# DLRM tower on one Trainium2 core: fifteen tables looked up by one-hot matmul instead of five, and pair products kept in four chunks instead of seven

## The chip, the cores and the metric

One core of one Trainium2 chip runs the kernel, compiled as one program. The metric is the device time of one execution in microseconds (us): the median over runs. The kernel before takes 226.08 us (three runs, 224.97 to 227.42).

## The reference

```python
# ids: (512, 26) int32; 26 tables of 1000, 1250, 12500 or 125000 rows x 128; dense: (512, 128)
e = stack([tbl_n[ids[:, n]] for n in range(26)], axis=1)           # (512, 26, 128)
combined = concatenate([dense[:, None, :], e], axis=1)               # 27 features per sample
interactions = einsum('bfd,bgd->bfg', combined, combined)            # 27 x 27 products per sample
z = concatenate([dense, interactions[:, iu, ju]], axis=1)            # the 351 pairs f < g
h = concatenate([z, dense], axis=1)                                  # 607 columns
h = maximum(h @ W_top1 + b_top1, 0); h = maximum(h @ W_top2 + b_top2, 0)   # 607x512, 512x256
y = h @ W_top3                                                       # (512, 1)
```

All of it is fp32.

## The kernel before

The batch of 512 is four tiles of 128 samples. Everything ends in `featT` (128 dims on the partitions, sample, feature), from which the products of one sample are one small matmul.

There are two ways into `featT`. **Gathered tables** (21 of 26): GpSimd issues one indirect DMA per tile and table (84 in all, L289), which fetches 128 rows to `gathered`; TensorE transposes them in groups of up to four tables (`fill`, L485), and ScalarE or VectorE copies the group to `featT` (L307, L385). **One-hot tables** (5, of 1000 rows): the table lies in SBUF as 125 partitions with 8 rows each; for each of the 8 chunks a one-hot matrix (row number equals id) is made, and table chunk times one-hot, accumulated in PSUM over the chunks, is the looked-up embedding, already transposed, for all 512 samples. To be exact, the table is split in a high part (ScalarE, L333) and a low part (VectorE, L424), so each chunk is two matmuls (L462, L464). The ids are spread over the partitions: by a small matmul (L475) for VectorE, which compares three chunks in an instruction (L418, six chunks of eight), and by DMA for ScalarE, which does the other two with an Abs (L347) and a Relu (L352). ScalarE then copies the result to `featT` (L301).

SP issues the loads in its program's order (`load_table`, L253, waits for a free one of three buffers); GpSimd issues the gathers without waiting for anything but the ids.

Then come five stages: tiles 0 to 2, and tile 3 in two (columns cut at chunk 5). In a stage, TensorE computes the 128 products of a tile (L511, four quadrants of the array), VectorE and ScalarE copy them from PSUM to `zT` (L391, L314), in seven chunks of at most 122 rows, and layer 1 multiplies `zT` by `w_inter` (L539) and adds the dense part (L534, which reads `featT` at feature 0). Layers 2 and 3 (L563, L573) follow a tile later. Each fp32 matmul shows as two instructions in the profile, so 128 products are 256. The order of TensorE's work is written out at the end of its program, with `BESIDE` blocks of layer 1 of the stage before placed between quarters of the products. Engines meet only in semaphores.

## Time and profile before

| | us |
|---|---|
| time, median of 3 runs | 226.08 (224.97 to 227.42) |
| profiled execution, span from first to last instruction | 152.9 |
| profiled execution, its own time | only its span is shown |
| TensorE matmuls busy | 115.3 (75%) |
| weight loads busy | 95.1 (62%) |
| VectorE busy | 51.1 (33%) |
| ScalarE busy | 49.8 (33%) |
| GpSimd busy | 83.9 (55%) |
| bytes moved by DMA | 12.82 MB, mean 84 GB/s |

A busy time is the sum of an engine's instructions; what the busy share hides is that the span has two parts with different limits, which the views by stretch and the chain of waits tell apart. In a row of instructions, `out<-in` names the tiles, `x40` the count; behind the bar stand busy us, mean ns of one, and the idle time of the engine before them with what ended it.

### The profile page before, as it was taken

To read this page: it belongs to the slowest core of one execution; us is meant where nothing else is said; L and a number is where in the kernel's file an instruction comes from. 1 tells how busy PE (TensorE), PEld (TensorE's weight loads), DVE (VectorE), ACT (ScalarE), POOL (GpSimd) and SP (SyncE) were. 2 spreads that over 40 slices of the span, in tenths; PEclk is the share of its full clock that TensorE was granted. 3 is DMA by queue.
4 is the path that set the end of the run, shared out by engine and by line. 5 is a ranking of instruction groups with operands and counts; after the bars stand their busy time and mean duration, and the time that the engine had idled before them with its cause. 6 is when DMAs were issued, how large, how long until landed. Compare 5 with 4: busy or idle time off the path is not lost.

```text
span 152.9 us, 3980 instructions
## 1 busy us (share of the span) xinstructions
PE 115.3 (75%) x1789; PEld 95.1 (62%) x1789; DVE 51.1 (33%) x88; ACT 49.8 (33%) x98; POOL 83.9 (55%) x91
## 2 busy tenths in 40 slices
PE   0339401999379965599899899958999949995993
PEld 0127201677157654486788788647989739994691
DVE  6665600076457810712103800234500405104100
ACT  5045203368499840703000800204500106104011
POOL 4777777777787877777777777777710000000000
PEclk9999955569978999557999999997799996999659
DMA  1684447999644322221222221122210000000000
GB/s 43 151 192 164 166 164 227 270 248 238 172 166 167 119 53 57 50 57 51 55 53 56 58 51 51 51 56 56 60 30 0 0 9 0 4 4 0 4 0 1
DMA packets 5547, 12.82 MB, mean 84 GB/s; under 512 B 2025, under 2 KB 3049, under 8 KB 5277
## 3 DMA queue, kind: packets, MB, share of 16 engines
q0 software_dynamic: 2688, 5.51, 15.2%
q1 hardware_dynamic: 2832, 7.05, 15.0%
q8 instruction: 14, 0.23, 0.7%
q14 instruction: 3, 0.02, 0.0%
q10 hardware_dynamic: 10, 0.01, 0.0%
HBM read 12.56 MB, written 0.00 MB: 82 GB/s over the span
## 4 chain that ended last, share of the span: by engine, by line
PE 57%; DMA 25%; DVE 7%; issue 7%; ACT 2%; SPq 1%; ACTq 0%
DMA table_sb<-tbl 25%; PE h_ps L539 17%; PE gram_ps L511 9%; PE h_ps L563 7%; PE h_ps L534 6%; PE fill_ps L485 5%; DVE zT L391 5%; PE gram_ps L462 3%; PE gram_ps L539 3%; PE gram_ps L464 3%; DVE featT L385 2%; ACT featT L301 1%; PE gram_ps L534 1%; PE h_ps L573 1%; DVE h L396 1%
## 5 line engine op out<-in xcount | busy, mean ns | idle before, releaser
L289 POOL DMA_INDIRECT gathered<-tbl,ids_sb x84 | 83.1, 989 | 26.9 <-issue 25.3
L539 PE MATMUL h_ps<-zT,w_inter_sb 122*128 122x128 f32 (+1 forms) x196 | 29.2, 295 | 1.6 <-DVE zT L391 1.6
L539 PEld LDWEIGHTS h_ps<-zT,w_inter_sb 122*128 122x128 f32 (+1 forms) x196 | 27.3, 203 | 4.7 <-DVE zT L391 1.9
L462 PE MATMUL gram_ps<-onehot,table_hi 125*128 125x512 f32 x40 | 20.8, 519 | 4.8 <-DVE table_lo L424 4.7
L314 ACT ACTIVATE zT<-gram_ps 26x224 f32<-26x224 f32 (+4 forms) x40 | 12.1, 302 | 37.7 <-PE gram_ps L511 36.9
L418 DVE TENSOR_TENSOR onehot<-h_ps,rowno 125x1536 fp32r<-125x1536 f32 x10 | 17.5, 1755 | 17.8 <-PE gram_ps L464 16.9
L511 PE MATMUL gram_ps<-featT 128*26 128x26 f32 (+2 forms) x1280 | 15.5, 188 | 9.0 <-issue 5.8
L391 DVE COPY zT<-gram_ps 26x224 f32<-26x224 f32 (+4 forms) x40 | 12.9, 323 | 24.6 <-PE gram_ps L511 23.5
L511 PEld LDWEIGHTS gram_ps<-featT 128*26 128x26 f32 (+1 forms) x1280 | 13.2, 102 | 11.9 <-issue 7.5
L464 PE MATMUL gram_ps<-onehot,table_lo 125*128 125x512 f32 x40 | 19.6, 490 | 0.0
L307 ACT ACTIVATE featT<-fill_ps 128x512 f32<-128x512 f32 (+1 forms) x14 | 9.1, 656 | 26.4 <-PE fill_ps L485 26.4
L385 DVE COPY featT<-fill_ps 128x512 f32<-128x512 f32 (+1 forms) x10 | 6.0, 605 | 31.4 <-PE fill_ps L485 31.4
L485 PE MATMUL fill_ps<-ident,gathered 128*128 128x128 f32 x84 | 13.4, 302 | 3.7 <-ACT featT L307 3.4
L462 PEld LDWEIGHTS gram_ps<-onehot,table_hi 125*128 125x128 f32 x40 | 10.2, 254 | 9.6 <-DVE table_lo L424 5.4
L485 PEld LDWEIGHTS fill_ps<-ident,gathered 128*128 128x128 f32 x84 | 10.8, 157 | 5.7 <-issue 5.1
L563 PE MATMUL h_ps<-h,w_sb 128*128 128x128 f32 x64 | 13.2, 390 | 0.1
L563 PEld LDWEIGHTS h_ps<-h,w_sb 128*128 128x128 f32 x64 | 12.3, 295 | 0.4 <-issue 0.2
L534 PE MATMUL h_ps<-featT,w_dsum 128*128 128x128 f32 x28 | 10.4, 463 | 2.5 <-DVE zT L391 2.5
L464 PEld LDWEIGHTS gram_ps<-onehot,table_lo 125*128 125x128 f32 x40 | 10.1, 253 | 2.3
L347 ACT ACTIVATE id_off<-oh_ids_sb,minus_rowno 125x512 f32<-125x512 int32 x10 | 7.2, 717 | 10.8 <-DMA oh_ids_sb<-oh_ids 10.6
L333 ACT ACTIVATE table_hi<-table_sb 125x1024 fp32r<-125x1024 f32 x5 | 5.3, 1053 | 12.6 <-DMA table_sb<-tbl 12.6
L424 DVE TENSOR_TENSOR table_lo<-table_sb,table_hi 125x1024 fp32r<-125x1024 f32 x5 | 6.1, 1223 | 6.2 <-ACT table_hi L333 6.2
(33 smaller groups left out, 55.5 us busy)
## 6 DMA issues: line engine op xcount, KB each, us to landing
table_sb<-tbl SPq DMA_DIRECT2D x5, 500.0 KB
w_inter_sb<-w_inter SPq DMA_DIRECT2D x1, 1792.0 KB, 29.9
gathered<-tbl,ids_sb POOLq DMA_INDIRECT x84, 3.8
oh_ids_sb<-oh_ids SPq DMA_DIRECT2D x1, 1000.0 KB
w_dense_sb<-w_dense SPq DMA_DIRECT2D x1, 512.0 KB, 25.0
w_sb<-w SPq DMA_DIRECT2D x1, 512.0 KB, 26.8
dense_sb<-dense SPq DMA_DIRECT2D x1, 256.0 KB, 23.2
oh_ids_sb<-oh_ids SPq DMA_DIRECT2D x1, 250.0 KB
```

The costliest lines, as they stand in the source:

```text
L289: pool.indirect_dma_start(out=gathered[:, t, pos - GATHERED[0], :], out_offset=None, in_=tables[table], in_offset=bass.IndirectOffsetOnAxi ...
L307: nc.scalar.activation(group_target(t, g), group_source(n % 2, g), ACT.Copy) \
L314: nc.scalar.activation(z_target(stage, j, q), z_source(stage, j, q), ACT.Copy) \
L391: nc.vector.tensor_copy(z_target(stage, j, q), z_source(stage, j, q)).then_inc(z_dve, 1)
L418: nc.vector.tensor_tensor(onehot[:, c:c + DVE_STEP, :], oh_ids_ps(k).unsqueeze(1).to_broadcast(of_step), rowno[:, c:c + DVE_STEP].unsqueez ...
L462: nc.tensor.matmul(lookup_ps(k), table_hi[:, k % 2, rows], onehot[:, c, :], start=(c == 0), stop=False)
L464: last = nc.tensor.matmul(lookup_ps(k), table_lo[:, k % 2, rows], onehot[:, c, :], start=False, stop=(c == RCHUNKS - 1))
L485: last = nc.tensor.transpose(fill_ps[n % 2][:, i * P:(i + 1) * P], gathered[:, t, pos - GATHERED[0], :], ident[:, :])
L511: last = nc.tensor.matmul(gram_ps[stage % 2][QUAD * j:QUAD * j + rows, col + first:col + rows], featT[:, b, 0:rows], featT[:, b, 1 + first ...
L534: nc.tensor.matmul(layer1_ps(t, n), w_dsum[:, units], featT[:, tile, 0], start=(n == 0 or (t == LAST and n == N1 // 2)), stop=False, skip_ ...
L539: last = nc.tensor.matmul(layer1_ps(t, n), w_inter_sb[0:k, c, units], zT[0:k, c, tile], start=False, stop=(c == CHUNKS - 1), skip_group_ch ...
L563: last = nc.tensor.matmul(h2_ps[:, n * P:(n + 1) * P], w2_sb[:, k, n * P:(n + 1) * P], h1[:, k, :], start=(n == 0 and k == 0), stop=(k == ...
```

## The change

Fifteen tables instead of five are looked up by one-hot matmul: the twelve of 1000 rows (8 chunks) and three of 1250 rows (10 chunks), all padded with zeros by the host to 128 partitions. The remaining eleven are gathered, 44 gathers instead of 84, and a gather is held back until a count of looked-up chunks is reached (`chunks_ahead`). The ids are spread by DMA for each table ahead of its rows; ScalarE makes a second copy with one added, and VectorE compares two chunks in one instruction on SBUF operands alone (`compare_two`). Lookups are written to PSUM in pairs of banks and copied to `featT` in pairs of features (`pair_to_featT`); `featT` has 32 slots, five of them second copies of features (`COPIED`). The products of a sample are 32 rows by 27 columns, and because some rows are there twice, the 351 pairs are picked with two copies per quadrant (`BELOW`, then `ABOVE` over its first `CUT` rows) into four full chunks of `zT` instead of seven; `w_inter` is laid out to match. The dense input has its own `denseT`. Tile 3 is no longer cut in two stages; TensorE's order behind the lookups is a written list; layer 3 runs once for three tiles and once for the last.

```diff
+LAST = TILES - 1
...
+ONEHOT_TABLES = (0, 1, 3, 6, 7, 8, 11, 12, 13, 14, 21, 15, 16, 18, 20)
+LARGER = (7, 13, 21)
+ONEHOTS = len(ONEHOT_TABLES)
...
+SHORT, LONG = 8, 10
...
+RAW_BUFS = 3
...
+GATHERS_AHEAD = 4
+CHUNKS_A_GATHER = 3
...
+PAIR_SLOTS = ((0, 1), (5, 6), (24, 25), (4, 7), (9, 10), (8, 11), (23, 26))
+COPIED = (2, 4, 7, 9, 10)
...
-ONEHOT_TABLES = (0, 1, 3, 6, 8)
...
-ROWS = 1000
-RCHUNKS = 8
-RPARTS = ROWS // RCHUNKS
-DVE_CHUNKS = 6
-DVE_STEP = 3
...
-LAST_CUT = 5
-STAGES = [(t, 0, CHUNKS) for t in range(LAST)] + [(LAST, 0, LAST_CUT), (LAST, LAST_CUT, CHUNKS)]
...
-BESIDE = (3, 0, 0, 2)
...
+CUT = (3, 9, 16, 22)
+ABOVE = ((0, 6, 7, 13), (3, 5, 8, 10), (11, 12, 15, 16), (14, 17, 18, 21))
+BELOW = ((13, 19, 20, 26), (22, 23, 24, 25), (0, 1, 3, 4), (5, 6, 8, 9))
+ZCOPIES = 2 * len(CUT)
...
+AFTER_LOOKUP = [[], [], [(0, 0)], [], [], [], [], [(0, 1)], [], [(0, 2)], [], [], [], [], []]
...
+def dve_chunks(k):
...
+    if row_chunks(k) == LONG:
+        return LONG - 2
+    return SHORT if k > 0 and k % 2 == 1 else SHORT - 2
...
+def chunks_ahead(n):
+    return min((n - GATHERS_AHEAD) * CHUNKS_A_GATHER, row_chunks_to(ONEHOTS))
...
-                if k >= 3:
-                    sp.wait_ge(hi_ready, k - 2)
-                    sp.wait_ge(lo_ready, k - 2)
-                rows = tables[ONEHOT_TABLES[k]].rearrange("(p c) d -> p (c d)", c=RCHUNKS)
-                sp.dma_start(table_sb[:, k % 3, :], rows).then_inc(table_in[k], 16)
+                if k >= RAW_BUFS:
+                    sp.wait_ge(hi_ready, 2 * (k - RAW_BUFS + 1))
+                    sp.wait_ge(lo_ready, 2 * (k - RAW_BUFS + 1))
+                rows = tables[ONEHOT_TABLES[k]].rearrange("(p c) d -> p (c d)", c=row_chunks(k))
+                sp.dma_start(table_sb[k % RAW_BUFS][:, 0:table_cols(k)], rows).then_inc(table_in[k], 16)
+            def spread_ids(k):
+                if k >= IDS_BUFS:
+                    sp.wait_ge(id_off_ready, act_chunks_to(k - IDS_BUFS + 1))
+                    sp.wait_ge(onehot_dve, dve_chunks_to(k - IDS_BUFS + 1))
+                sp.dma_start(ids_all[:, k % IDS_BUFS, 1, :], oh_ids[k].partition_broadcast(P)) \
+                    .then_inc(ids_all_in[k % IDS_BUFS], 16)
...
-            load_table(0)
...
-            sp.dma_start(oh_ids_sb[:, 0, :], oh_ids[0].partition_broadcast(RPARTS)).then_inc(oh_ids_in[0], 16)
+            rows = tables[ONEHOT_TABLES[0]].rearrange("(p c) d -> p (c d)", c=SHORT)
+            sp.dma_start(table_sb[0][:, 0:FIRST], rows[:, 0:FIRST]).then_inc(table_0_in, 16)
+            sp.dma_start(table_sb[0][:, FIRST:table_cols(0)], rows[:, FIRST:]).then_inc(table_in[0], 16)
+            spread_ids(1)
             load_table(1)
...
             for k in range(2, ONEHOTS):
+                spread_ids(k)
                 load_table(k)
-            sp.dma_start(w_dense_sb[:, :, :], w_dense).then_inc(w_dense_in, 16)
+                if k == 4:
+                    sp.dma_start(dense_sb[:, :, :], dense).then_inc(dense_in, 16)
+                if k == 5:
+                    sp.dma_start(w_dense_sb[:, :, :], w_dense).then_inc(w_dense_in, 16)
+                    sp.dma_start(small_sb[:, :], small).then_inc(small_in, 16)
...
+                        n = t * GATHERED + pos - FIRST_GATHERED
+                        if n > GATHERS_AHEAD:
+                            pool.wait_ge(chunk_done, chunks_ahead(n))
                         pool.indirect_dma_start(
-                            out=gathered[:, t, pos - GATHERED[0], :], out_offset=None, in_=tables[table],
+                            out=gathered[:, t % ROW_BUFS, pos - FIRST_GATHERED, :], out_offset=None, in_=tables[table],
                             in_offset=bass.IndirectOffsetOnAxis(ap=ids_sb[:, col:col + 1], axis=0),
                         ).then_inc(rows_in[t][g], 16)
...
+            def pair_to_featT(pair):
+                act.wait_ge(lookup_done, 2 * (pair + 1) + 1)
+                if PAIR_SLOTS[pair][0] in COPIED:
+                    copy = FEATS + COPIED.index(PAIR_SLOTS[pair][0])
+                    nc.scalar.activation(pair_target(pair, (copy, copy + 1)), lookup_pair(pair), ACT.Copy) \
+                        .then_inc(copied, 1)
+                nc.scalar.activation(pair_target(pair, PAIR_SLOTS[pair]), lookup_pair(pair), ACT.Copy) \
+                    .then_inc(lookup_read, 2)
...
+            def products_to_zT(t, half):
+                j = 2 + half
+                act.wait_ge(gram_ready, t + 1)
+                for q in range(4):
+                    nc.scalar.activation(z_target(t, j, q, QUAD), z_source(t, j, BELOW[q], QUAD), ACT.Copy) \
+                        .then_inc(z_act, 1)
+                for q in range(4):
+                    act.wait_ge(z_act, ZCOPIES * (2 * t + half) + q + 1)
+                    nc.scalar.activation(z_target(t, j, q, CUT[q]), z_source(t, j, ABOVE[q], CUT[q]), ACT.Copy) \
+                        .then_inc(z_act, 1)
...
+            def compare_last(k):
+                if k == 0:
+                    act.wait_ge(ids_0_ready, 1)
+                if k >= 2:
+                    act.wait_ge(lookup_done, k - 1)
+                for c in range(dve_chunks(k), row_chunks(k)):
+                    nc.scalar.activation(onehot[k % 2][:, c, :], ids_all[:, k % IDS_BUFS, 1, :], ACT.Abs,
+                                         bias=row_number(minus_rowno, k, c)).then_inc(id_off_ready, 1)
+                act.wait_ge(id_off_ready, act_chunks_to(k + 1))
+                act_part = onehot[k % 2][:, dve_chunks(k):row_chunks(k), :]
+                nc.scalar.activation(act_part, act_part.bitcast(fp32), ACT.Relu, bias=1.0, scale=-1.0) \
+                    .then_inc(onehot_act, row_chunks(k) - dve_chunks(k))
+            def next_ids(k):
+                act.wait_ge(ids_all_in[k % IDS_BUFS], ids_loads(k))
+                nc.scalar.activation(ids_all[:, k % IDS_BUFS, 0, :], ids_all[:, k % IDS_BUFS, 1, :], ACT.Relu, bias=1.0) \
+                    .then_inc(next_ids_ready, 1)
...
-                for c in range(DVE_CHUNKS, RCHUNKS):
-                    done = k * (RCHUNKS - DVE_CHUNKS) + c - DVE_CHUNKS
-                    if done:
-                        act.wait_ge(onehot_act, done)
-                    nc.scalar.activation(id_off[:, :], oh_ids_sb[:, k, :], ACT.Abs,
-                                         bias=minus_rowno[:, c:c + 1]).then_inc(id_off_ready, 1)
-                    if k > 0:
-                        act.wait_ge(onehot_used, RCHUNKS * (k - 1) + c + 1)
-                    act.wait_ge(id_off_ready, done + 1)
-                    nc.scalar.activation(onehot[:, c, :], id_off[:, :], ACT.Relu, bias=1.0, scale=-1.0) \
-                        .then_inc(onehot_act, 1)
+                if dve_chunks(k) < row_chunks(k):
+                    compare_last(k)
+                if k + 1 < ONEHOTS:
+                    next_ids(k + 1)
                 if k + 1 < ONEHOTS:
                     high_parts(k + 1)
...
+                    act.wait_ge(filled[0], 1)
+                    nc.scalar.activation(denseT[:, :], fill_ps[0][:, :], ACT.Copy).then_inc(denseT_ready, 1)
+                    nc.scalar.activation(featT[:, :, FEATS], fill_ps[0][:, :], ACT.Copy).then_inc(copied, 1)
+                    nc.scalar.activation(featT[:, :, DENSE_SLOT], fill_ps[0][:, :], ACT.Copy).then_inc(fill_read[0], 1)
...
+                elif k % 2 == 1:
+                    pair_to_featT((k - 3) // 2)
...
+            def compare_two(k, c):
+                nc.vector.tensor_scalar(onehot[k % 2][:, c:c + 2, :], ids_all[:, k % IDS_BUFS, :, :],
+                                        row_number(rowno, k, c + 1), None, ALU.is_equal).then_inc(onehot_dve, 2)
+            def low_parts(k):
+                dve.wait_ge(hi_ready, 2 * (k + 1))
+                cols = slice(0, table_cols(k))
+                nc.vector.tensor_tensor(table_lo[k % SPLIT_BUFS][:, cols], table_sb[k % RAW_BUFS][:, cols],
+                                        table_hi[k % SPLIT_BUFS][:, cols].bitcast(fp32), ALU.subtract) \
+                    .then_inc(lo_ready, 2)
...
-                    nc.vector.tensor_tensor(onehot[:, c:c + DVE_STEP, :],
-                                            oh_ids_ps(k).unsqueeze(1).to_broadcast(of_step),
-                                            rowno[:, c:c + DVE_STEP].unsqueeze(2).to_broadcast(of_step),
-                                            ALU.is_equal).then_inc(onehot_dve, DVE_STEP)
...
+                    nc.tensor.matmul(lookup_ps(k), table_hi[k % SPLIT_BUFS][:, rows], onehot[k % 2][:, c, :],
+                                     start=(c == 0), stop=False).then_inc(chunk_done, 1)
+                    last = nc.tensor.matmul(lookup_ps(k), table_lo[k % SPLIT_BUFS][:, rows], onehot[k % 2][:, c, :],
+                                            start=False, stop=(c == row_chunks(k) - 1))
+                last.then_inc(lookup_done, 1)
...
+                        b = t * P + j * QUAD + s
+                        last = nc.tensor.matmul(product_ps(t)[QUAD * j:QUAD * (j + 1), SLOTS * s:SLOTS * s + FEATS],
+                                                featT[:, b, :], featT[:, b, 0:FEATS], start=True, stop=True)
...
+                    nc.tensor.matmul(layer1_ps(t, n), w_dense_sb[:, 0, n * P:(n + 1) * P], denseT[:, t * P:(t + 1) * P],
+                                     start=(n == 0 or t == LAST and n == N1 // 2), stop=False, skip_group_check=True)
...
-                for c in range(c0, c1):
-                    k = chunk_rows(c)
-                    last = nc.tensor.matmul(layer1_ps(t, n), w_inter_sb[0:k, c, units], zT[0:k, c, tile],
-                                            start=False, stop=(c == CHUNKS - 1), skip_group_check=True)
...
+                    last = nc.tensor.matmul(layer1_ps(t, n), w_inter_sb[:, c, n * P:(n + 1) * P],
+                                            zT[:, c, t * P:(t + 1) * P],
+                                            start=False, stop=(c == ZCHUNKS - 1), skip_group_check=True)
...
-                                            start=(k == 0), stop=(k == N2 - 1))
+                    last = nc.tensor.matmul(fill_ps[bank][0:1, at:at + tiles * P], w3_sb[:, k:k + 1],
+                                            h2[:, k, first * P:(first + tiles) * P],
...
+                for t, g in AFTER_LOOKUP[k]:
+                    fill(t, g)
+            fill(1, 0)
+            products(0, 0)
+            products(0, 1)
+            layer1_dense(1)
+            fill(1, 1)
+            fill(1, 2)
+            products(0, 2)
+            fill(2, 0)
+            products(0, 3)
+            fill(2, 1)
+            fill(2, 2)
+            products(1, 0)
+            layer1_dense(0)
+            products(1, 1)
+            fill(3, 0)
+            fill(3, 1)
+            products(1, 2)
+            layer1(0, 0)
+            products(1, 3)
+            layer1(0, 1)
+            products(2, 0)
+            layer1(0, 2)
+            layer1(0, 3)
+            products(2, 1)
+            fill(3, 2)
+            products(2, 2)
+            layer1(1, 0)
+            layer1(1, 1)
+            products(2, 3)
+            layer2(0)
+            products(LAST, 0)
+            layer1(1, 2)
+            products(LAST, 1)
+            layer1(1, 3)
+            layer1_dense(LAST)
+            products(LAST, 2)
+            layer1_dense(2)
+            products(LAST, 3)
+            layer1(2, 0)
+            layer1(2, 1)
+            layer1(2, 2)
+            layer2(1)
+            layer1(2, 3)
+            layer1(LAST, 0)
+            layer1(LAST, 1)
+            layer2(2)
+            layer1(LAST, 2)
+            layer1(LAST, 3)
+            layer2_last(0)
+            layer2_last(1)
+            layer3(0, LAST)
+            layer3(LAST, 1)
```

## Rows read from the trace of the kernel before

**Rows 1.** The core: its span and mean granted clock.

```profile
core 0: 152.9 us, clock 0.866
```

**Rows 2.** Stretch, us, busy (count) of PE, PEld, DVE, ACT, POOL; clock, DMA share, GB/s.

```profile
30.00:40.00 10.00, 9.46 (x36) 6.97 (x34) 6.41 (x4) 5.66 (x7) 7.78 (x8) 0.82 1.01 240
...
0.00:54.20 54.20, 32.58 (x106) 23.63 (x107) 27.54 (x20) 27.54 (x38) 40.47 (x46) 0.84 0.63 175
54.20:152.90 98.70, 82.72 (x1685) 71.42 (x1683) 23.58 (x68) 22.24 (x61) 43.42 (x46) 0.88 0.14 34
```

**Rows 3.** Chain that ended last: start us, us, what.

```profile
1.92 38.28 DMA table_sb<-tbl x2
...
48.20 0.23 PE gram_ps L464
...
49.35 0.44 PE fill_ps L485 x4
...
66.08 3.28 PE h_ps L539 x14
...
87.72 1.76 PE h_ps L539 x14
89.48 0.68 PE h_ps L534 x2
...
105.19 3.61 PE h_ps L563 x16
...
151.05 0.28 DVE y_sb L401
```

**Rows 4.** Instructions by line: busy us, mean ns, idle before.

```profile
L289 POOL DMA_INDIRECT gathered<-tbl,ids_sb x84 | 83.1, 989 | 26.9 <-issue 25.3 <-DMA ids_sb<-ids 1.6
...
L418 DVE TENSOR_TENSOR onehot<-h_ps,rowno 125x1536 fp32r<-125x1536 f32 x10 | 17.5, 1755 | 17.8 <-PE gram_ps L464 16.9 <-PE h_ps L475 0.9
...
L347 ACT ACTIVATE id_off<-oh_ids_sb,minus_rowno 125x512 f32<-125x512 int32 x10 | 7.2, 717 | 10.8 <-DMA oh_ids_sb<-oh_ids 10.6
...
L301 ACT ACTIVATE featT<-gram_ps 128x512 f32<-128x512 f32 x5 | 6.0, 1202 | 1.2 <-PE gram_ps L464 1.2
...
L333 ACT ACTIVATE table_hi<-table_sb 125x1024 fp32r<-125x1024 f32 x5 | 5.3, 1053 | 12.6 <-DMA table_sb<-tbl 12.6
...
L424 DVE TENSOR_TENSOR table_lo<-table_sb,table_hi 125x1024 fp32r<-125x1024 f32 x5 | 6.1, 1223 | 6.2 <-ACT table_hi L333 6.2
...
L404 DVE MEMSET zT<- 128x2688 f32 x1 | 2.3, 2298 | 1.4 <-PEq L648 1.4
```

**Rows 5.** The same, each shape apart.

```profile
L307 ACT ACTIVATE featT<-fill_ps 128x512 f32<-128x512 f32 x10 | 6.9, 692 | 26.4 <-PE fill_ps L485 26.4
...
L391 DVE COPY zT<-gram_ps 20x160 f32<-20x160 f32 x8 | 2.5, 316 | 3.9 <-PE gram_ps L511 3.7
...
L391 DVE COPY zT<-gram_ps 26x64 f32<-26x64 f32 x4 | 0.9, 215 | 8.9 <-PE gram_ps L511 8.8
```

**Rows 6.** DMA queues: packets, MB, share of 16 engines; one issue group, us to landing.

```profile
q0 software_dynamic: 2688, 5.51, 15.2%
q1 hardware_dynamic: 2832, 7.05, 15.0%
...
gathered<-tbl,ids_sb POOLq DMA_INDIRECT x84, 3.8
```

**Rows 7.** TensorE's matmuls by time: start us, us, then idle before.

```profile
99.74 2.38 PE L511 MATMUL gram_ps<-featT 128*26 128x26 f32 x161 [0.59 <-DVE featT L385]
103.82 1.37 PE L511 MATMUL gram_ps<-featT 128*26 128x26 f32 x95 [1.70 <-issue]
...
124.98 0.75 PE L511 MATMUL gram_ps<-featT 128*20 128x20 f32 x70 [2.29 <-issue]
```

**Rows 8.** GpSimd and VectorE by time: start us, us.

```profile
9.38 1.62 POOL L289 DMA_INDIRECT gathered<-tbl,ids_sb  x1 [0.30 <-issue]
...
8.96 1.23 DVE L424 TENSOR_TENSOR table_lo<-table_sb,table_hi 125x1024 fp32r<-125x1024 f32 x1 [1.90 <-ACT table_hi L333]
```

More of the change, by code:

```diff
@@ L85, in groups_of_stage @@
-def groups_of_stage(stage):
-    t, c0, c1 = STAGES[stage]
-    return [g for g, group in enumerate(GROUPS) if 4 * c0 < group[-1] <= last_position(c1)]
-def chunk_rows(c):
-    return QUAD * (min(4, COLS - 4 * c) - 1) + FEATS - 1
-def tower(nc, dense, ids, oh_ids, tables, w_inter, w_dense, b1, w2, b2, w3, out):
+LAST = TILES - 1
[3 more added lines that the diff above has]
+SHORT, LONG = 8, 10
+FIRST = SHORT // 2 * DIM
@@ L97, in tower, with quads @@
+def quads(cols):
+    a, b, c, d = cols
+    if a + d == b + c:
+        return a, c - a, b - a
+    raise ValueError(cols)
+def tower(nc, dense, ids, oh_ids, tables, w_inter, w_dense, small, w2, out):
     fp32, fp32r, i32 = mybir.dt.float32, mybir.dt.float32r, mybir.dt.int32
@@ L128, in tower @@
+        onehot = [sb(f"onehot{i}", [P, buffer_chunks(i, 2), BATCH], fp32r) for i in range(2)]
+        dense_sb = sb("dense_sb", [P, TILES, DIM])
+        gathered = sb("gathered", [P, ROW_BUFS, GATHERED, DIM])
+        featT = sb("featT", [P, BATCH, SLOTS])
+        denseT = sb("denseT", [P, BATCH])
+        zT = sb("zT", [P, ZCHUNKS, BATCH])
+        ids_row = zT[0:1, 0, :].bitcast(i32)
+        w_inter_sb = sb("w_inter_sb", [P, ZCHUNKS, HID1])
         w_dense_sb = sb("w_dense_sb", [P, 2, HID1])
-        w_dsum = sb("w_dsum", [P, HID1])
@@ L137, in tower @@
+        h2 = table_sb[0][:, 0:N2 * BATCH].rearrange("p (n b) -> p n b", n=N2)
+        y_sb = denseT[0:1, :]
         ident = sb("ident", [P, P])
@@ L542, in layer1 @@
                     last.then_inc(h1_psum, 1)
-            def layer1_before(stage):
-                layer1_start(stage)
-                for n in range(N1 - BESIDE[stage]):
-                    layer1(stage, n)
+                elif n == N1 - 1:
+                    last.then_inc(h1_psum_last, 1)
             def layer2(t):
@@ new lines, in layer2, with layer2_last @@
+                last.then_inc(h2_psum, 1)
+            def layer2_last(half):
+                if half == 0:
+                    pe.wait_ge(h2_ready, N2 * LAST)
+                    pe.wait_ge(h1_ready, N1 * LAST + N1 // 2)
+                else:
+                    pe.wait_ge(h1_act, N1 // 2)
+                for n in range(N2):
+                    for k in range(half * N1 // 2, (half + 1) * N1 // 2):
+                        last = nc.tensor.matmul(layer2_ps(LAST, n), w2_sb[:, k, n * P:(n + 1) * P],
+                                                h1[:, LAST % 2, k, :], start=(k == 0), stop=(k == N1 - 1))
+                    if half == 1:
+                        last.then_inc(h2_psum, 1)
@@ new lines, in _ @@
+            layer1(2, 0)
[12 more added lines that the diff above has]
+            layer3(LAST, 1)
+def first_layer_layout(w1):
+    w = np.zeros((P, ZCHUNKS, HID1), w1.dtype)
+    placed = set()
+    for q in range(4):
+        for c in range(ZCHUNKS):
+            for r in range(QUAD):
+                column = ABOVE[q][c] if r < CUT[q] else BELOW[q][c]
+                other = r if r < FEATS else COPIED[r - FEATS]
+                lo, hi = sorted((FIELD_AT[column], FIELD_AT[other]))
+                if lo != hi and (lo, hi) not in placed:
+                    placed.add((lo, hi))
+                    pair = lo * FEATS - lo * (lo + 1) // 2 + (hi - lo - 1)
+                    w[QUAD * q + r, c] = w1[DIM + pair]
+    assert len(placed) == FEATS * (FEATS - 1) // 2
```

573 lines of the change are left out of this document (296 added, 277 removed).

## The prediction

> **What bounds the kernel now.** I read the span first: 152.9 us from first to last instruction, with a mean granted clock of 0.866 [rows 1]. No time of this profiled execution other than its span is shown; the median of the three runs is 226.08 us, so 73.2 us lie around the span. The sum below is made against 152.9 us, and I leave the 73.2 us as they are (the runs alone spread over 2.4 us).
>
> The busy times by stretch [rows 2] split the span in two. Up to 54.2 us five tables are looked up and the engines are half idle: TensorE is busy for 32.58 of 54.2 us. Then come 98.7 us of tiles, in which TensorE is busy for 82.72 us. The chain of waits [rows 3] says who sets each part: until 40 us it is the table loads (38.28 us), behind 54 us nearly only TensorE. So phase one is bound by transfers, though the DMA engines have a share of only 0.63 in it [rows 2] (tables of 0.5 MB, 125 partitions each, one after another), phase two by TensorE's own instructions. GpSimd, with 84 gathers at 1.29 us each (0.99 busy and 0.30 between) [rows 4], is beside both.
>
> **Phase one after the change.** Ten more tables go through the lookup. I cost it by four engines and take the largest.
>
> TensorE: 12 tables of 8 chunks and 3 of 10 are 126 chunks, two matmuls each, 252 instead of 80. At the full clock one is 0.23 us [rows 3], so 58.5 us. The first few at half clock cost 1.5 us, and 15 transposes at 0.11 us (four in 0.44 us) 1.7 us: 62 us.
>
> ScalarE [rows 4, 5]: nine tables have two chunks compared here, each two L347 (0.72) and one pass over 1024 elements (L333, 1.05): 22 us. Fourteen second copies of the ids, each at most like L347 (512 elements, 0.72): 10 us. Fourteen high parts at 1.05, three of them a quarter longer: 15 us. Eight pair copies: nearest rows are L301, 512 elements in separate places, 1.20 us, and L307, 512 elements in runs of four, 0.69 us. If the run costs, a pair is 1.2; if each element costs, 2.4; I take 1.5, since most pairs are neighbours: 12 us. One single, two dense copies, a contiguous one and three fills: 6 us. Sum 65 us (63 to 72).
>
> VectorE [rows 4]: fourteen low parts at 1.23 and longer: 18 us. The 51 compares of two chunks are a new form: one input stream in SBUF, 1024 elements. Above stands L424, two SBUF streams and 1024 elements, 1.22 us. Below, the same row at half: it reads 2048 values where the compare reads 1024; with its 0.15 us of fixed part (L418: 1536 elements in 1.755, L424: 1024 in 1.223) that is 0.69 us. The memset L404 (2688 elements in 2.298 us, or 0.95 us for 1024) lies between. I take 0.69: 35 us, and with the single compares of table 0 56 us in all (71 by the memset, 84 by L424). The Trainium skill ("VectorE: DVE Perf Modes", the perf-mode tier table) puts an fp32 tensor_scalar between SBUF tensors at two elements per cycle, and tensor_tensor at one; no run here shows it yet, and by it the compares are 35 us, else 63.
>
> Transfers [rows 6]: 8.26 MB of tables, 3.67 MB of ids for 14 tables, 0.77 MB of dense inputs, and some 40 gathers of 64 KB, 15.3 MB. At the 240 GB/s of the stretch in which the engines were full [rows 2] 64 us. By the packet time of the queues (7.05 MB in 15.0% of 16 x 152.9 us is 307 GB/s; gathers 237 GB/s) 53 us. The 128 partitions and padded tables keep all engines in use; SP waits for the buffer of three tables before, so loads are at most two tables ahead.
>
> GpSimd: a gather each three chunks (six matmuls, 1.4 us) against 1.29 us now: it keeps pace, if it isn't held up.
>
> Four near-equal loads, 56 to 65 us, coupled through two onehot buffers and three table buffers. At each odd table ScalarE waits for the lookup before, then copies the pair, while the next compare waits behind it. I add 5 us (bounds 0 and 15). The first matmul comes at about 6.5: half a table is issued at about 1.2 us and takes the 3.8 us of a gather to land [rows 6], then 0.6 us of high part and 0.7 of low part. Lookups end at 6.5 + 65 + 5 = 76.5 us, against 54.2: **22 us lost**.
>
> **Phase two after the change.** Per TensorE instruction: layer 1 is 0.126 us at the full clock and 0.23 at half (14 in 1.76 or in 3.28 us), layer 2 the same pair (16 in 3.61 us, at half clock) [rows 3].
> - Products: 4 tiles of 256 instead of 5 stages. A stage is 3.75 us (2.38 + 1.37) and an issue gap of 1.70 [rows 7]: 15.0 us. Such gaps stand in three of five stages (1.70 and 2.29 are the ends), none where products stood between layer 1; I count two, 3.6 us (0 to 9). The 32 rows and 27 columns instead of 26 I cost at nothing: a stage with 20 columns has the same pace (70 in 0.75 us).
> - Layer 1: 16 blocks of 4 chunks, 128 instructions, 16.1 us, where 7 chunks took 28. Dense part: 32 instructions that now read denseT with step one, 0.126 each, 4.0 us; today's L534 reads featT with a step and takes 0.34 (two in 0.68) [rows 3], which would make 10.9. I take 4.0, as zT is read the same way.
> - Layer 2: 64 at 0.126, 8.1. Fills: 33 transposes left, 3.6. Layer 3 once for three tiles and once for the last: 2.1.
>
> That is 52.5 us. Clock dips: behind the stages with a gap layer 2 runs at half clock, 16 x (0.226 - 0.126), 1.6 us lost; I count three, 4.8. Reading the last lookup 0.7, the end (0.28 and 1.6 until the output) 1.9. Sum 60 us (53 to 69) against 98.7: **39 us won**.
>
> The copies to zT grow to 16 per engine and tile, of 128 elements: at most the 0.316 us of the form of 160 [rows 5], 5 us per tile. They hide beside 12 to 13 us of TensorE work per tile, because the order puts a tile's layer 1 behind the next tile's products; uncovered, at the last tile, they cost 2 us, which the 60 holds. The second copy of a quadrant waits for the first, four copies back, so nothing idles.
>
> Span 76.5 + 60 = 136.5 us, 16.4 less. **Forecast 226.1 - 16.4 = 209.7 us.** Lowest by the bounds: lookups end at 68.5, tail 53: 194.7.
>
> **Rivals.**
> - *VectorE and GpSimd shut each other out* (slower). Today's rows show one direction: the gather at 9.38 us takes 1.62 where the mean is 0.99, and L424 ran until 10.19 [rows 8]. After the change nearly all VectorE work of phase one reads SBUF alone. If every gather stops VectorE as well, 44 x 0.95 = 42 us join its 56 us: lookups end at 104.5, and the time is 237.7. It decides from 0.7 us stopped per gather, where VectorE passes 86 us. Against it: that L424 took 1.23, as the mean of all five, with gathers running beside them. The Trainium skill ("SBUF — State Buffer", who interferes with whom) says that a vector instruction in a two-port mode and GpSimd exclude each other fully, and that descriptors of GpSimd's DMAs then can't be written; the rows agree for the direction they show. Chance 0.09.
> - *Only the gathers fall behind.* With 2.5 us per gather 28 are done by 76 us, and the rest at 1.29 end 20 us later, when tile 3 wants them: 3 us. At 4 us per gather, 27 remain for 35 us, and tile 3 is 19 us late: 229. Chance 0.06, half of it costly.
> - *The compare runs at L424's rate.* VectorE 84 us, lookups end at 92.5 us, time 225.7: same. The memset row speaks for part of that: 215. Chance 0.08.
> - *The tail stays at half clock.* 224 layer instructions at 0.10 us more are 22 us, 17 beyond my dips: 227; half of that 218. For it: the clock in the tail is 0.88 today with dips behind each gap. Against: products are split in quarters among other work. Chance 0.07.
>
> That the change does what it says is certain in its counts (84 gathers to 44, 5 tables to 15).
>
> **How the numbers follow.** My forecast has 0.70, reaching from 194.7 to about 219. About 1% is what a measurement of this kernel can tell from no change. Faster by more: 0.70 and 0.12 of the milder halves of the last three, 0.82. Within 1%: 0.07. Slower: 0.09 and 0.02, 0.11. The range takes in the late gathers, 194 to 229.
>
> **What would show it.** Lookup matmuls 0.23 us apart with few waits, ending at 70 to 80 us; compares at 0.6 to 0.75 us; gathers of 1 to 2 us; half the layer-1 time; at most three clock dips behind the lookups. The forecast is wrong if the compare takes over 0.95 us, if VectorE instructions get longer whenever a gather runs, if the last table lands behind 72 us, or if TensorE waits for zT in the tail.

## The result, and the profile after

The changed kernel takes **122.31 us** (four runs, 122.06 to 123.26). Beside it, in the session that also gave the time of before shown above, the kernel before took 226.29 us (224.97 to 227.42), a ratio of 0.541 [0.538, 0.545]. In every later run the kernel before took 150.7 to 155.1 us (32 executions on three chips, medians 152.9, 153.1, 153.1 and 152.3). The ratio of the repeat under these conditions is **0.804 [0.791, 0.817]**, 122.93 against 153.10 us. Both intervals lie clear of 1. The second ratio is the one that the traces explain: the profiled execution of before in the first session already had a span of 152.9 us, but its own time is not on record, so nothing shows what the executions of 226 us spent more.

The spans: 119.5 us after (its own time is 122.08), 152.9 before, so 33.4 us less; forecast was 16.4 us less. By stretch, the lookups end 16.4 us later than before (70.6 against 54.2 us) and the tail behind them is 49.8 us shorter (48.9 against 98.7). The remaining 70.6 us of the first difference are in neither of these two spans.

The core's line, its span and mean granted clock, answering to [rows 1]:

```profile
core 0: 119.5 us, clock 1.000
```

The page of the changed kernel (busy time in tenths over 40 slices, the clock in tenths, GB/s):

```profile
PE   0299899999999999999979999869999999999993
DVE  2563998999969969999769923299387485485110
ACT  5875897993999899996998031395393492492231
POOL 3776786777747777777657600000000000000000
PEclk9999999999999999999999999999999999999999
GB/s 73 202 343 389 350 302 359 351 254 176 318 292 203 235 261 219 163 286 278 389 225 51 44 22 5 5 0 5 5 5 5 5 5 0 8 5 0 0 0 1
```

TensorE is busy from the first lookup to the end and its granted clock never leaves 1.0, where before it was 0.866 [rows 1]. The same by stretch, answering to [rows 2]: lookups, tail (all that follows the last lookup), and the lookups from their first matmul on (columns as there).

```profile
0.00:70.60 70.60, 64.02 (x270) 50.70 (x271) 57.80 (x78) 56.13 (x72) 49.43 (x52) 1.00 0.76 245
70.60:119.50 48.90, 45.17 (x1290) 40.48 (x1288) 26.40 (x86) 23.93 (x80) 0.00 (x0) 1.00 0.01 4
...
5.87:70.60 64.73, 63.25 (x269) 50.38 (x270) 55.45 (x72) 52.29 (x66) 46.22 (x42) 1.00 0.78 255
```

The third line shows what bounds the lookups: TensorE is idle for 1.5 of 64.7 us. (The run with thirteen tables, below, agrees: 40 lookup matmuls less end the lookups 7.5 us earlier.) Groups of the page by line, answering to [rows 4, 5]:

```profile
L345 POOL DMA_INDIRECT gathered<-tbl,ids_sb x44 | 48.6, 1104 | 18.1 <-issue 10.4
L532 DVE TENSOR_SCALAR onehot<-ids_all,rowno 128x1024 fp32r<-128x1024 int32 x52 | 36.2, 755 | 0.0
L538 DVE TENSOR_TENSOR table_lo<-table_sb,table_hi 128x1024 fp32r<-128x1024 f32 (+1 forms) x14 | 17.8, 1274 | 7.7 <-issue 4.9
L360 ACT ACTIVATE featT<-gram_ps 128x1024 f32<-128x1024 f32 x6 | 6.8, 1133 | 2.5 <-issue 1.9
L498 DVE COPY zT<-gram_ps 32x128 f32<-32x128 f32 x32 | 9.0, 283 | 8.8 <-PE gram_ps L654 7.9
```

And pieces of the chain of waits (start us, us, what), answering to [rows 3, 7]: the first lookup matmuls, then products, layer 1, layer 2 and the end. `issue` is time in which the engine waited for nothing that the profile shows; on TensorE the text calls it a gap.

```profile
5.87 0.76 PE gram_ps L617
6.63 0.43 PE gram_ps L619
...
11.90 0.23 PE gram_ps L617
...
78.09 0.39 PE gram_ps L654 x32
78.48 1.03 issue
...
94.12 1.98 PE h_ps L693 x16
96.10 0.69 PE gram_ps L654 x50
96.79 1.09 PE h_ps L679 x8
...
112.13 1.79 PE gram_ps L679 x16
113.92 1.87 PE h_ps L706 x16
115.79 1.83 PE fill_ps L722 x8
```

Layer 1 runs at 0.112 us an instruction (16 in 1.79), a quarter of the products takes 0.69 us, and no block of a layer takes twice its time, as one of layer 2 did before, 16 in 3.61 us [rows 3]; such a stretch at half the granted clock is called a dip.

### The profile page after: what moved, and what is told of

Read it like the earlier page. It is cut to its first block, busy times and chain, and to the rows that moved or that the text cites. A ratio compares the mean times of both kernels' runs of the same rounds, so it can differ in the third digit from the quotient of the medians.

```text
span 119.5 us, 3689 instructions
## 1 busy us (share of the span) xinstructions
PE 109.2 (91%) x1557; PEld 91.2 (76%) x1557; DVE 84.2 (70%) x164; ACT 80.1 (67%) x152; POOL 49.4 (41%) x52
## 4 chain that ended last, share of the span: by engine, by line
PE 85%; ACT 5%; issue 4%; DVE 3%; DMA 1%; DVEq 0%; ACTq 0%
PE gram_ps L617 23%; PE gram_ps L619 22%; PE h_ps L679 10%; PE gram_ps L654 10%; PE h_ps L693 5%; PE fill_ps L630 5%; PE gram_ps L679 3%; PE h_ps L669 3%; PE h_ps L706 2%; PE fill_ps L722 2%; DMA zT<-oh_ids 1%; DVE table_lo L538 1%; ACT onehot L415 1%; ACT featT L358 1%; ACT featT L360 1%
## 5 line engine op out<-in xcount | busy, mean ns | idle before, releaser
L345 POOL DMA_INDIRECT gathered<-tbl,ids_sb x44 | 48.6, 1104 | 18.1 <-issue 10.4
L617 PE MATMUL gram_ps<-onehot,table_hi 128*128 128x512 f32 x126 | 51.7, 410 | 3.8 <-DVE table_lo L545 2.4
L619 PE MATMUL gram_ps<-onehot,table_lo 128*128 128x512 f32 x126 | 50.6, 402 | 0.0
L532 DVE TENSOR_SCALAR onehot<-ids_all,rowno 128x1024 fp32r<-128x1024 int32 x52 | 36.2, 755 | 0.0
L617 PEld LDWEIGHTS gram_ps<-onehot,table_hi 128*128 128x128 f32 x126 | 24.6, 195 | 11.5 <-issue 3.6
L619 PEld LDWEIGHTS gram_ps<-onehot,table_lo 128*128 128x128 f32 x126 | 24.7, 196 | 5.0
L538 DVE TENSOR_TENSOR table_lo<-table_sb,table_hi 128x1024 fp32r<-128x1024 f32 (+1 forms) x14 | 17.8, 1274 | 7.7 <-issue 4.9
L431 ACT ACTIVATE table_hi<-table_sb 128x1024 fp32r<-128x1024 f32 (+1 forms) x14 | 15.3, 1095 | 2.0 <-DMA table_sb<-tbl 1.3
L654 PE MATMUL gram_ps<-featT 128*32 128x27 f32 x1024 | 12.6, 195 | 1.8 <-issue 1.6
L679 PE MATMUL h_ps<-zT,w_inter_sb 128*128 128x128 f32 x96 | 13.0, 284 | 0.0
L415 ACT ACTIVATE onehot<-ids_all,minus_rowno 128x512 fp32r<-128x512 int32 x16 | 10.6, 713 | 0.0
L424 ACT ACTIVATE ids_all<-ids_all 128x512 int32<-128x512 int32 x14 | 8.7, 620 | 0.7 <-issue 0.7
```

Source lines behind the costliest of these rows:

```text
L345: pool.indirect_dma_start(out=gathered[:, t % ROW_BUFS, pos - FIRST_GATHERED, :], out_offset=None, in_=tables[table], in_offset=bass.Indir ...
L415: nc.scalar.activation(onehot[k % 2][:, c, :], ids_all[:, k % IDS_BUFS, 1, :], ACT.Abs, bias=row_number(minus_rowno, k, c)).then_inc(id_of ...
L431: nc.scalar.activation(table_hi[k % SPLIT_BUFS][:, 0:table_cols(k)], table_sb[k % RAW_BUFS][:, 0:table_cols(k)], ACT.Copy).then_inc(hi_rea ...
L532: nc.vector.tensor_scalar(onehot[k % 2][:, c:c + 2, :], ids_all[:, k % IDS_BUFS, :, :], row_number(rowno, k, c + 1), None, ALU.is_equal).t ...
L538: nc.vector.tensor_tensor(table_lo[k % SPLIT_BUFS][:, cols], table_sb[k % RAW_BUFS][:, cols], table_hi[k % SPLIT_BUFS][:, cols].bitcast(fp ...
L617: nc.tensor.matmul(lookup_ps(k), table_hi[k % SPLIT_BUFS][:, rows], onehot[k % 2][:, c, :], start=(c == 0), stop=False).then_inc(chunk_don ...
```

## The experiments

Ratios are to the kernel before, timed on the same chip at the same time. The theory to test: the lookups are bound by TensorE because the tables now come fast, and the tail shrank because layer 1 has four chunks, the products run in quarters, and gaps and dips are gone. The rivals: VectorE and GpSimd hinder each other; the time before was set by its 84 gathers; the time outside the span is part of the kernel.

**The kernel before again.** No edit.

> The kernel before, unchanged, to see its time beside its own span. Theory A (some 73 us of its time lie outside the span, between the span's ends and the time's): time about 226 us, span about 153 us again. Theory B (the profiled execution shown was an unusually short one): a span of 220 us or more in an execution of 226 us, and the stretch that grew is to be seen in the trace.

Measured: 154.32 us (153.55 and 155.09), span 151.7 in the run of 153.55. So 1.8 us lie around its span, not 73. What made it 226 us in the first session did not return and stays open; it isn't shown either whether those executions had a longer span or more time around it.

**The changed kernel again.** No edit.

> The changed kernel unchanged, beside the kernel before on the same chip. Theory A (the 226 us of the kernel before were a condition of those executions, not of the kernel): before stays at 152 to 153 us as in the last runs, this one at 122 to 123, ratio 0.80. Theory B (the kernel before alternates between 153 and 226 us): some executions of before come at 226 us again.

Measured: 122.93 us (121.56 to 123.38), 0.804 [0.791, 0.817], within 1% of the 122.31 of the first session. What lengthened the kernel before there did not touch this one.

**Padded tables, alone in the kernel before.**

```diff
-ROWS = 1000
+ROWS = 1024        # the five one-hot tables get 24 rows of zeros: 128 partitions
```

> The kernel before with its five one-hot tables padded with zero rows to 128 partitions, nothing else. If loads of 125 partitions cost the 73 us outside the span, the time falls to about 150 us. If they only slow the loads, as the span's chain of waits has it (38 us of table loads), the last table lands some 10 to 20 us earlier, the span is 135 to 145 us and the 73 us stay.

Measured: 141.55 us, 0.929 [0.916, 0.943]. Three stretches tell why; first of the kernel before, then of the padded one (columns as in [rows 2]):

```profile
10.00:14.00 4.00, 3.77 (x9) 2.99 (x10) 2.55 (x3) 2.70 (x4) 3.08 (x4) 1.00 0.48 165
14.00:18.00 4.00, 3.04 (x9) 2.02 (x7) 2.57 (x3) 1.06 (x1) 3.08 (x4) 1.00 0.48 166
18.00:22.00 4.00, 0.00 (x0) 0.00 (x0) 1.38 (x1) 0.00 (x0) 3.09 (x4) 0.73 0.48 168
```

```profile
10.00:14.00 4.00, 4.00 (x15) 3.09 (x15) 2.67 (x2) 2.31 (x4) 3.08 (x4) 1.00 1.05 359
14.00:18.00 4.00, 4.00 (x20) 3.02 (x19) 3.26 (x3) 3.88 (x6) 3.09 (x4) 1.00 0.94 319
18.00:22.00 4.00, 4.00 (x21) 3.04 (x20) 3.50 (x4) 3.78 (x6) 3.08 (x4) 1.00 1.06 435
```

With 125 partitions half the time of the DMA engines is unused at 165 GB/s; with 128 they are full at 320 to 435 GB/s, and TensorE no longer waits. The Trainium skill ("DMA: Bandwidth & Descriptors", section "Why a DMA increments its semaphore by 16 and not by 1") says that such a transfer uses the largest number of engines up to 16 that divides the outermost dimension of both its sides: 16 for 128, and by the rule 5 for 125. The trace agrees, roughly: 5 of 16 are 0.31, and gathers alone have a share of 0.22 at 54 GB/s (60 to 100 us of the kernel before), together 0.53, where 0.48 was measured. The last low part (L424) then starts at 28.5 instead of 48.6 us, but the time falls by 11.3 us only, because TensorE now waits for gathered rows (the waits of the padded kernel: total us, times, longest):

```profile
PEld fill_ps L485 <- DMA gathered<-tbl,ids_sb: 9.3, 5, 4.4
```

**The changed kernel without padding.**

```diff
+TP = 125
-                sp.dma_start(table_sb[k % RAW_BUFS][:, 0:table_cols(k)], rows).then_inc(table_in[k], 16)
+                sp.dma_start(table_sb[k % RAW_BUFS][0:TP, 0:table_cols(k)], rows).then_inc(table_in[k], 16)
...  (high parts, low parts and lookup matmuls over 0:TP as well)
```

> The changed kernel with its fifteen tables unpadded, 125 partitions of 8 or 10 rows. If 125 partitions use fewer DMA engines, a table takes 6 us or more alone instead of 2 to 3 and the lookups become bound by it: 15 tables of 0.5 MB at about 80 GB/s are 100 us, so lookups end at 100 to 110 us instead of 70.6 and the span grows by 30 to 40 us. If the number of partitions doesn't matter, the span stays within 2 us of 119.5. If 125 partitions are what costs time outside the span, the time exceeds the span by some 70 us.

Measured: 155.15 us, 1.019 [1.009, 1.029]: **no faster than the kernel before**, rather some 2% slower, and 32 us over the changed kernel. Its chain, by line:

```profile
DMA table_sb<-tbl 45%; PE h_ps L680 8%; PE gram_ps L655 8%; ACT table_hi L432 4%; DVE table_lo L539 4%; PE h_ps L694 4%; PE gram_ps L618 3%; PE gram_ps L620 3%; PE fill_ps L631 3%; PE gram_ps L680 2%; PE h_ps L670 2%; PE h_ps L707 1%; PE fill_ps L723 1%; PE gram_ps L670 1%; DVE onehot L533 0%
```

Fifteen tables pay only because they are padded.

**Half the gathers in the kernel before.**

```diff
-            for t in range(TILES):
+            for t in range(2):          # tiles 2 and 3 read the rows of tiles 0 and 1
```

> The kernel before with 42 gathers instead of 84: tiles 2 and 3 use the gathered rows of tiles 0 and 1 (so the scores of half the batch are another's). If the time outside the span comes with the gathers, it falls from 73 to near 2.6 us (by a threshold between 44 and 84) or to about 36 us (in proportion); if not, it stays at 73. The span should move by under 5 us, since GpSimd is beside the path.

Measured: 151.44 us, 0.994 [0.988, 0.999]. In the kernel as it was, the gathers are beside the path: half of them are worth 0.6%.

**Gathers not held back.**

```diff
-                        if n > GATHERS_AHEAD:
-                            pool.wait_ge(chunk_done, chunks_ahead(n))
```

> The changed kernel with its gathers issued as fast as they go, not held to the count of looked-up chunks. If GpSimd and VectorE shut each other out, more gathers meet the compares early: compares grow from a mean of 755 ns, lookups end later than 70.6 us, time up by 2 us or more. If only the gathers are held up (they wait for the VectorE instruction in progress), gathers take 1.5 to 2 us each and end before 60 us, and the time stays within 1% of 122.3.

Measured: 122.57 us, 0.806 [0.795, 0.818], the same as with the hold. Gathers 1095 ns, compares 751 ns on average. The edit changed little: the last gather starts at 63.8 instead of 67.1 us, so gathers run beside the lookups nearly all the time in both kernels. The durations say more. No compare is stopped: all 52 take 0.73 to 0.82 us in the changed kernel, and the subtractions of 1024 elements (L538) keep to 1.21 to 1.23 us. In the other direction one wait shows. Six of the 44 gathers take 1.37 to 2.11 us where the shortest take 0.94, and each begins while a subtraction runs and ends 0.81 to 0.83 us behind its end; the edited kernel has six such gathers too (1.29 to 1.95 us). Two of them in the changed kernel, with the subtraction of each:

```profile
22.41 2.11 POOL L345 DMA_INDIRECT gathered<-tbl,ids_sb  x1 [0.62 <-issue]
22.21 1.48 DVE L538 TENSOR_TENSOR table_lo<-table_sb,table_hi 128x1280 fp32r<-128x1280 f32 x1
...
43.88 1.94 POOL L345 DMA_INDIRECT gathered<-tbl,ids_sb  x1 [0.30 <-issue]
43.77 1.22 DVE L538 TENSOR_TENSOR table_lo<-table_sb,table_hi 128x1024 fp32r<-128x1024 f32 x1 [1.01 <-issue]
```

So VectorE is not held up by GpSimd. GpSimd is held up by the subtractions, which read two tiles in SBUF, some 4.4 us over the six gathers (10.0 us less six times 0.94), and hardly by the compares (nearly all gathers beside them take 0.94 to 1.10 us). As GpSimd sets neither the lookups nor the tail, that costs the kernel nothing. [rows 8] show the same pair: that gather ends 0.81 us behind L424.

**Products of a tile in one piece.**

```diff
-            products(0, 0)
-            products(0, 1)
+            for part in range(4):
+                products(0, part)
...  (the same for tiles 1 to 3; layer blocks behind them)
```

> The changed kernel with TensorE's order behind the lookups such that the four quarters of a tile's products stand together, as in the kernel before, and layer 1 behind them. If the split products are what kept the clock full and the issue gaps short, each of four tiles gets a gap of 1 to 2 us and some a stretch at half clock: tail from 48.9 to 55 to 60 us, time 128 to 133. If the four-chunk layout alone did it, the tail stays within 2 us.

Measured: 127.98 us, 0.841 [0.830, 0.852], 5 us over the changed kernel. TensorE's matmuls by time show four gaps, 8.5 us against 1.8:

```profile
74.86 0.78 PE L654 MATMUL gram_ps<-featT 128*32 128x27 f32 x67 [2.30 <-issue]
83.42 1.02 PE L654 MATMUL gram_ps<-featT 128*32 128x27 f32 x96 [2.07 <-issue]
96.00 0.38 PE L654 MATMUL gram_ps<-featT 128*32 128x27 f32 x19 [2.25 <-issue]
105.79 0.83 PE L654 MATMUL gram_ps<-featT 128*32 128x27 f32 x73 [1.91 <-issue]
```

Of a tile's 256 instructions 67, 96, 19 and 73 come behind the gap, so it stands after 160 to 237 of them. The clock was 0.986 on average: one dip came behind the second gap (0.70 from 85 to 90 us), none behind the other three. So a gap in the products alone does not bring a dip.

**The dense part from featT, with a step.**

```diff
-                    nc.tensor.matmul(layer1_ps(t, n), w_dense_sb[:, 0, n * P:(n + 1) * P], denseT[:, t * P:(t + 1) * P],
+                    nc.tensor.matmul(layer1_ps(t, n), w_dense_sb[:, 0, n * P:(n + 1) * P], featT[:, t * P:(t + 1) * P, DENSE_SLOT],
```

> The changed kernel with the dense part of layer 1 read from feature slot 2 of featT (a step of 128 bytes) instead of denseT. At the 0.34 us per instruction that L534 had in the kernel before against 0.11 to 0.14 with step one, 32 instructions cost 6.5 to 7.5 us more: time 129 to 130. If the step costs nothing, 122.3.

Measured: 123.87 us, 0.813 [0.803, 0.822], about 1 us more and within the intervals. Eight instructions in a row take 1.93 instead of 1.09 us, 0.24 each; the 0.34 of [rows 3] was not reached. Over the four blocks that is 3.4 us more in the chain; why the time grew by less isn't shown.

**Seven chunks again.** The first three chunks of layer 1 are multiplied twice, so its result differs.

```diff
-                for c in range(ZCHUNKS):
+                for c in (0, 1, 2, 0, 1, 2, 3):
```

> The changed kernel with seven matmuls instead of four in each block of layer 1 (chunks 0 to 2 are added twice, so the scores are others). At 0.112 us per instruction 96 more are 10.8 us, if TensorE bounds the whole tail: 133. If waits hide part of layer 1, less than 8 us.

Measured: 132.02 us, 0.868 [0.856, 0.880]: 9 us more; its tail is 10.4 us longer (59.3 against 48.9) for 96 more instructions. TensorE bounds the tail, and the four chunks are worth about 10 us.

**Full chunks of 128 rows in the kernel before.** The rows beyond 58 or 122 hold zeros.

```diff
 def chunk_rows(c):
-    return QUAD * (min(4, COLS - 4 * c) - 1) + FEATS - 1
+    return P
```

> The kernel before with layer 1 multiplying all 128 rows of each of its seven chunks (zeros in the rows that were left out), instead of 122 rows and 58 in the last. If the chunk of 58 rows is what makes 14 instructions take 1.76 us where 10 without it take 1.12, a block falls to about 1.57 us and 16 blocks give back 3 us: 149.5 to 150. If rows don't matter, 153.

Measured: 143.96 us, 0.943 [0.933, 0.953]: 9 us where 3 were expected. The chain, before and then with full rows:

```profile
110.08 1.76 PE h_ps L539 x14
...
130.50 1.12 PE h_ps L539 x10
...
141.28 1.82 PE h_ps L539 x8
143.10 2.90 PE gram_ps L539 x8
145.99 3.72 PE h_ps L563 x16
```

```profile
106.26 1.56 PE h_ps L539 x14
...
125.16 1.12 PE h_ps L539 x10
...
135.94 1.13 PE h_ps L539 x8
137.07 0.89 PE gram_ps L539 x8
137.96 1.94 PE h_ps L563 x16
```

Sixteen blocks at 0.20 us are the 3 us. They come with the chunk of 58 rows: the ten instructions over the first five chunks take 1.12 us in both kernels, so 122 rows cost as much as 128. The four over the last two chunks, of 122 and 58 rows, fall from 0.64 to 0.44 us. Of the other 6 us the end of the kernel shows 4.5: its last three blocks take 3.96 us instead of 8.44, and the granted clock there is 1.00 instead of 0.62 (columns as in [rows 2], before and then with full rows):

```profile
141.00:150.00 9.00, 8.42 (x32) 6.67 (x32) 1.05 (x4) 1.02 (x4) 0.00 (x0) 0.62 0.01 2
135.00:141.00 6.00, 4.35 (x36) 3.98 (x36) 1.62 (x7) 1.97 (x8) 0.00 (x0) 1.00 0.01 3
```

Multiplying more zeros made the kernel faster. Why the clock then stays up isn't shown: TensorE stands idle for some 2 us ahead of these blocks in both.

**Layer blocks beside the products of every stage, in the kernel before.**

```diff
-BESIDE = (3, 0, 0, 2)
+BESIDE = (3, 3, 3, 2)
```

> The kernel before with three blocks of layer 1 between the quarters of the products in every stage (BESIDE 3, 3, 3, 2 instead of 3, 0, 0, 2). If products that stand together cost an issue gap of about 2 us and a stretch of half clock behind it, two stages give back 3 us each: 145 to 149. If the gaps are only moved, 152 to 153.

Measured: 146.55 us, 0.958 [0.949, 0.967], 6.6 us less.

**The three small edits together** (padded, full rows, blocks beside), and the same with half the gathers.

> The kernel before with the three small edits that helped it singly: its five tables padded to 128 partitions (11.6 us less alone), layer 1 over all 128 rows of every chunk (9.2 less), BESIDE 3, 3, 3, 2 (6.6 less). If these sit in different parts of the path they add up: 153.1 - 27.4 = 125.7 us, and fifteen tables and four chunks are then worth only some 3 us over it. The padding acts before 54 us, so it is separate; the other two both touch the clock of the layer blocks and may share their gain: 130. Rival: the 84 gathers (about 1.28 us each, the last rows in at some 113 us) become the bound as the tail gets earlier; then it stays at 132 to 138 and TensorE waits for gathered rows in the tiles 2 and 3.

Measured: 138.86 us, 0.910 [0.902, 0.917]: 13.4 us less, half of the 27.1 that they gave singly. TensorE waits for rows, and the chain says so:

```profile
PEld fill_ps L485 <- DMA gathered<-tbl,ids_sb: 14.7, 6, 4.6
```

```profile
POOL gathered L289 45%; PE h_ps L539 11%; PE gram_ps L511 6%; DVE zT L391 5%; PE h_ps L534 5%; PE gram_ps L539 2%; DMA gathered<-tbl,ids_sb 2%; PE h_ps L563 1%; DMA ids_sb<-ids 1%; PE fill_ps L485 1%; PE gram_ps L534 1%; DVE featT L385 1%; DVE h L396 1%; PE h_ps L573 0%; ACT h L326 0%
```

> The three small edits, and only the 42 gathers of tiles 0 and 1 are issued; tiles 2 and 3 read the rows gathered for tiles 0 and 1 (so the output is not the reference's). If the gathers bound the padded kernel, this is faster than the kernel with the three edits alone by what TensorE waited for rows: 4 to 10 us. If TensorE's own work bounds it, no difference over 1 us. In the kernel before without the edits it made 0.6%.

Measured: 130.66 us, 0.856 [0.849, 0.863]: 8.2 us less than with all 84. So the gathers, harmless before, bound the kernel once the rest is mended. The larger number of one-hot tables takes this bound away: in the changed kernel the last of 44 gathers begins at 67.1 us, and TensorE never waits for rows.

**Thirteen tables.** The changed kernel with tables 7 and 21 gathered: 20 of 126 chunks less, 52 gathers.

```diff
-ONEHOT_TABLES = (0, 1, 3, 6, 7, 8, 11, 12, 13, 14, 21, 15, 16, 18, 20)
-LARGER = (7, 13, 21)
+ONEHOT_TABLES = (0, 1, 3, 6, 8, 11, 12, 13, 14, 15, 16, 18, 20)
+LARGER = (13,)
-CHUNKS_A_GATHER = 3
+CHUNKS_A_GATHER = 2
...  (slots, pairs and the order of the fills to match)
```

> The changed kernel with two of its tables of 1250 rows gathered instead of looked up: 13 one-hot tables, 106 chunks instead of 126, 52 gathers instead of 44, one more group of fills per tile. If TensorE bounds the lookups, 40 matmuls of 0.23 us less are 9.2 us, and 8 more transposes and their copies cost 1 to 2: 114 to 116 us. If GpSimd becomes the bound (52 gathers at 1.4 us end at 76 us, TensorE wants the last at about 80), tile 3 waits and the time is 117 to 121.

Measured: **116.48 us** (116.14 to 117.22), 0.766 [0.758, 0.773]: the fastest here, 6 us less than with fifteen (whose ratio is 0.804). The lookups end at 63.1 instead of 70.6, and the gathers at 74, still ahead of the tiles that read them:

```profile
0.00:63.10 63.10, 55.35 (x232) 43.74 (x233) 48.88 (x67) 51.96 (x69) 48.28 (x51) 1.00 0.76 243
63.10:114.00 50.90, 46.28 (x1295) 41.47 (x1293) 25.76 (x86) 25.04 (x82) 8.50 (x9) 1.00 0.06 16
```

## Why the prediction was wrong

The direction was right and the time was wrong, 209.7 against 122.3 us. The step that failed is the first: "so 73.2 us lie around the span. The sum below is made against 152.9 us, and I leave the 73.2 us as they are". It took the difference between a span of one execution and the times of others for a fixed part of the kernel, which the change would leave alone. The runs show no such part: time less span is 1.8 us for the kernel before in its repeat, and 2.6 us for the changed kernel in the very session that had before at 226 us. What the 73.2 us were stays open. A span and a median of other executions that differ by half should have been a case of its own, with its own range; it had no chance at all. This step accounts for 70.4 of the 87.4 us of error.

The terms of the span account for the other 17.0, and they alone would have put the forecast wrong too. With 2.6 us around it, the forecast span of 136.5 gives 139.1 us, and its lowest bound, 121.5 (lookups at 68.5, tail of 53), gives 124.1; measured were 122.3. The sum had both halves too long, the lookups by 5.9 and the tail by 11.1 us.

Term by term:

- **Lookups, forecast 76.5, measured 70.6 us.** The bound was TensorE (63.25 of 64.73 us busy, forecast 62), not ScalarE at 65. ScalarE needed 56 us: a pair copy takes 1.13 us, where 1.5 was taken between 1.2 and 2.4, the second copy of the ids 0.62 instead of 0.72, and two chunks are compared there for eight tables and not for nine (16 instructions of L415). The coupling of 5 us was 1.5 us of idle TensorE. The first twelve matmuls at 0.43 instead of 0.23 us cost 2.4 us, where 1.5 was taken.
- **Transfers.** 64 us at 240 GB/s was no limit: slices reach 389 GB/s. That ceiling came from a stretch of the kernel before, with its transfers of 125 partitions, that had a DMA share of 1.01; here a share of 0.98 moved 362 GB/s (5.87 to 12 us). What held it lower there isn't shown. The text said that padding keeps all engines in use and gave it no price; it is worth 32 us (the run without padding), the largest single part of the change.
- **VectorE.** A compare takes 0.755 us (0.69 forecast), and there are 52, not 51. 1024 elements in 0.755 and 512 in 0.48 us leave 0.54 ns for each element more; the subtraction (L538, 1024 in 1.217 and 1280 in 1.482 us) has 1.04 ns. The Trainium skill ("VectorE: DVE Perf Modes", the perf-mode tier table) puts a tensor_scalar of fp32 in SBUF at twice the rate of a tensor_tensor. The trace agrees. The rival at L424's rate is refuted.
- **GpSimd.** A gather takes 1.10 us on average instead of 0.99 [rows 4]. The hold was unneeded, and VectorE was not lengthened. The rival of mutual exclusion held for one direction alone, and that one was free: gathers wait for the subtractions. The prediction counted its row of L424 as a case of a two-port mode, but L424 reads two tiles at the slower rate; beside the compares, which have the faster one, gathers hardly wait. The rival of late gathers is refuted: they end at 68 us.
- **Tail, forecast 60, measured 48.9 us.** The chain adds up to: products 11.6 (15.0), gaps 1.8 (3.6), layer 1 15.9 (16.1), dense 4.2 (4.0), layer 2 7.4 (8.1), fills 4.2 (3.6), layer 3 1.8 (2.1), dips none (4.8), ends 1.9 (2.6). The products were priced by a stage in one piece [rows 7], 3.75 us; split in quarters they take 2.8, in the kernel before too (51 in 0.66 us at 79.57 us). That the order splits them was used for the gaps and not for their pace.
- **Clock.** Three dips were counted and none came. In the kernel before the one at the end vanishes with full rows, and the run with four gaps has one; what the dips hang on was not isolated beyond that.
- **zT copies** of 0.27 to 0.28 us were hidden, as forecast.

Where the 30 us of the change come from, by single runs: padding 32 us within it, four chunks 9 to 10, split products 5, dense input about 1; they overlap and don't add up. Three edits of one or a few lines bring the kernel before to 138.9 us, nearly half of the way, and 8 us of the rest are the gathers.

## What to carry to other kernels

Before costing anything, ask why the time and the span of a kernel differ; where they can't be brought together, run the kernel again first, and until then give each reading a range of its own. Give tiles and transfers all 128 partitions, zeros included: for the table loads it was worth 11 us in one kernel and 32 in the other, and filling up the chunks of layer 1 was worth 9. When work moves from one path to another (gathers to matmuls), try the splits between: thirteen tables were 6 us faster than fifteen. No other number was run, so thirteen need not be the best.

## What was not expected of the hardware

- With table loads of 125 partitions (gathers beside them) the DMA share was 0.48 at 165 GB/s, with 128 it was 0.94 to 1.06 at 319 to 435 GB/s.
- An instruction of layer 1 took 0.126 us on average with chunks of 122 and 58 rows (14 in 1.76), 0.111 with 128 rows (14 in 1.56), and 0.112 with 122 rows alone (10 in 1.12).
- The first lookup matmuls took 0.43 us each for 5.5 us and then 0.23, while the granted clock of that stretch reads 1.00.
- A gather that begins early in a subtraction of two SBUF tiles ends 0.8 us behind it and takes up to 2.11 us, against 0.94; beside compares that have one SBUF tile as input it takes mostly 0.94 to 1.10 us. VectorE was lengthened by neither.
- Products of a whole tile in a row stop for 1.9 to 2.3 us after 160 to 237 of 256 instructions; in quarters of 64 between other matmuls only two stops remain, 0.56 and 1.03 us, both in the first tiles, where only transposes and the dense part stand between.
- The kernel before took 226 us in one session and 151 to 155 us in all others, though the one execution profiled in the first had a span of 152.9 us; the changed kernel took 122 to 123 us in both.
